# Value products on the transposes' banks, in two halves per head, and score tiles on three slots without a break

## The reference, cut to what matters

```
scores = q k^T                        per head: [256, 16] x [16, 4096]
p      = softmax(scores)              over the 4096 keys
pq     = round(p * 255 / max(p))      0..255, scale kept aside
vq     = round(v / scale_v)           -127..127, one scale per channel
o      = (pq @ vq) * scales           [256, 4096] x [4096, 16] per head
x      = x + o @ Wp + bp
```

## Time and profile before

| | us |
|---|---|
| median of 3 runs | 864.43 (859.89 to 864.85) |
| profiled execution | 861.99 |
| its span, first to last instruction | 860.0 |
| mean granted TensorE clock | 0.899 of full speed |
| busy in the span: PE, DVE, ACT, POOL | 688.4, 546.8, 416.0, 313.9 |

### The profile page before, as it was taken

How to read it: one execution, slowest core, us unless ns; L and a number is a source line. 1 busy time by engine, 2 the same in 40 slices (tenths; PEclk the granted TensorE clock), 3 DMA queues, 4 the chain that set the end, 5 groups by cost and what they waited for, 6 DMA issues and landing times. The chain is left out here.

```text
span 860.0 us, 14159 instructions
## 1 busy us (share of the span) xinstructions
PE 688.4 (80%) x4484; PEld 453.1 (53%) x4484; DVE 546.8 (64%) x834; ACT 416.0 (48%) x759; POOL 313.9 (36%) x232
## 2 busy tenths in 40 slices
PE   3817899978999998789974776867858676899997
PEld 1413445445776766567741444544535455576775
DVE  4487999955222222699986888788788883534222
ACT  2225555513222222355544888788788883313221
POOL 0081788850000000144432766666666662000000
PEclk9967999979999999899995889688797977999999
DMA  8554000003343430334437424224224200860000
GB/s 354 232 198 195 1 0 0 0 1 115 111 165 110 165 110 0 105 95 129 125 91 147 69 37 74 37 37 73 37 37 69 41 0 1 320 270 1 1 0 12
DMA packets 28652, 76.65 MB, mean 89 GB/s; under 512 B 3472, under 2 KB 21072, under 8 KB 22224
## 3 DMA queue, kind: packets, MB, share of 16 engines
q1 hardware_dynamic: 16080, 70.00, 27.7%
q10 hardware_dynamic: 12544, 6.29, 2.6%
HBM read 69.66 MB, written 6.62 MB: 89 GB/s over the span
## 5 line engine op out<-in xcount | busy, mean ns | idle before, releaser
L1468 DVE TENSOR_REDUCE d_nmax<-d_psum 128x1024 f32 (+1 forms) x128 | 155.4, 1217 | 15.1 <-PE d_psum L1595 12.0
L1605 PE MATMUL d_psum<-d_ident_f,d_rounded 128*128 128x128 f16 x1024 | 98.2, 253 | 64.5 <-ACT d_probsT L1551 62.6
L1605 PEld LDWEIGHTS d_psum<-d_ident_f,d_rounded 128*128 128x128 f16 x1024 | 81.4, 115 | 119.9 <-issue 82.6
L1595 PE MATMUL d_psum<-d_kst,d_qT 96*128 96x512 bf16 x256 | 98.4, 475 | 14.2 <-DMA d_kst<-kT_scratch 8.2
L430 POOL TENSOR_TENSOR b_h<-b_h,b_cb 128x1024 f32<-128x1024 f32 x32 | 84.5, 2642 | 31.4 <-DVE b_h L484 31.0
L1539 ACT ACTIVATE d_e<-d_psum,d_nmax 128x1024 f32<-128x1024 f32 x64 | 71.3, 1113 | 40.5 <-DVE d_nmax L1468 36.2
L1447 POOL TENSOR_SCALAR d_rounded<-d_e,d_lift 128x1024 f16<-128x1024 f32 x64 | 72.4, 1132 | 45.3 <-ACT d_lift L1543 40.9
L1447 POOL TENSOR_SCALAR d_rounded<-w_early,d_lift 128x1024 f16<-128x1024 f32 x64 | 71.6, 1119 | 40.4 <-ACT d_lift L1543 29.2
L484 DVE TENSOR_TENSOR_SCAN b_h<-b_dA,b_psum 128x1024 f32<-128x1024 f32 x32 | 73.0, 2285 | 7.6 <-PE b_psum L588 4.8
L544 ACT ACTIVATE b_dA<-b_dtT,b_A 128x248 f32<-128x248 f32 x128 | 53.6, 490 | 49.3 <-DVE b_h L484 43.3
L1539 ACT ACTIVATE w_early<-d_psum,d_nmax 128x1024 f32<-128x1024 f32 x64 | 71.2, 1114 | 8.6 <-DVE d_nmax L1468 8.5
(11 more groups left out here) (372 smaller groups left out, 1195.9 us busy)
## 6 DMA issues: line engine op xcount, KB each, us to landing
d_kst<-kT_scratch SPq DMA_DIRECT2D x96, 128.0 KB, 4.5
w_early<-in_w SPq DMA_DIRECT2D x8, 1152.0 KB, 5.2
w_late<-in_w SPq DMA_DIRECT2D x8, 1152.0 KB, 5.2
w<-in_w SPq DMA_DIRECT2D x8, 1088.0 KB, 19.9
b_cb<-c_scratch SPq DMA_DIRECT2D x4, 2048.0 KB, 7.1
kT_scratch<-k_kT ACTq DMA_DIRECT2D x16, 384.0 KB, 2.8
a_ctxT<-in_ctxT SPq DMA_DIRECT2D x2, 2048.0 KB, 11.8
a_ctx<-in_ctx SPq DMA_DIRECT2D x2, 2048.0 KB, 20.3
```

Of the source, the lines that this page charges most:

```text
L1468: nc.vector.tensor_reduce(nm[:, t, ds(m, 1), f:f + 1], quarter(j).unsqueeze(1), AX.X, ALU.max, negate=True).then_inc(nm_ready, 1)
L1595: last = nc.tensor.matmul(quarter(j)[:, c * 512:(c + 1) * 512], qT[0:QROWS, ds(m, 1), t * P:(t + 1) * P], kst[s][0:QROWS, at:at + 512], st ...
L1605: last = nc.tensor.transpose(turned[j % 2][:, c * P:(c + 1) * P], r[j][:, c * P:(c + 1) * P], ident16[:, :])
```

## The change

The value products move from banks 4 and 5 to the two banks of the turns: the uses of these banks now form a ring per head, T0, T1, V, T2, ..., T7, which alternates between them (nine uses, so the parity changes from head to head), and every use waits until the use two before it has been read. V is issued in two halves, tile 0 behind T1, tile 1 between S2 and T2, and `finish` reads 32 neighbouring columns of one bank, behind copy 2. The score units rotate over the three slots without regard to heads, so a score pair waits for the exp three units back. The slots and banks repeat after six heads, so the loop body holds six rounds and four rounds run ahead of it. `pT` and `vh` are f16. The scale of the values is computed in round 0 behind search 2. GpSimd fills a small constant tile (`unlift`) behind the all-reduce, and TensorE waits for that before its first score; the tile is read only by units turned by DMA, of which there are none here (`BY_DMA` is empty). SP's key loads are unrolled.

```diff
-    SLOT = (0, 1, 0, 1, 2, 0, 1, 2)
-    AV_BANK = 4
+    BY_DMA = ()
+    BY_PE = tuple(j for j in range(APH) if j // QT not in BY_DMA)
+    EVEN = tuple(j for j in BY_PE if j % 2 == 0)
+    ODD = tuple(j for j in BY_PE if j % 2 == 1)
+    RING = tuple(j for j in BY_PE if j < 2) + ("values",) + tuple(j for j in BY_PE if j >= 2)
     TURN_BANK = 6
+    UNROLL, LEAD = 6, 4
...
-        r = [sb(f"d_rounded{j}", [P, QUARTER], F16) for j in range(APH)]
-        pT = [sb(f"d_probsT{s}", [P, TC, NKC, P], BF16) for s in range(2)]
+        r = [sb(f"d_rounded{t}", [P, NK], F16) for t in range(TC)]
+        pT = [sb(f"d_probsT{s}", [P, TC, NKC, P], F16) for s in range(2)]
+        unlift = sb("d_minus_1024", [P, P], F16)
...
-            for m in range(2):
-                body(m, m, 0)
-            with eng.Fori(1, H // 2) as i:
-                for s in range(2):
-                    body(i * 2 + s, s, i)
+            for m in range(LEAD):
+                body(m, m, m // 2)
+            with eng.Fori(0, (H - LEAD) // UNROLL) as i:
+                for c in range(LEAD, LEAD + UNROLL):
+                    body(i * UNROLL + c, c, i * (UNROLL // 2) + c // 2)
...
+            slot = (c * APH + j) % 3
+            return flat[:, slot * QUARTER:(slot + 1) * QUARTER]
+
+        def turn_bank(c, use):
+            return TURN_BANK + (c * len(RING) + RING.index(use)) % 2
...
                 nc.gpsimd.partition_all_reduce(vall[:, :], g["vam"][:, :], P, RMAX).then_inc(vall_ready, 1)
+                nc.gpsimd.memset(unlift[:, :], -HALF_ULP_ONE).then_inc(ident_ready, 1)
...
+                def vector_head(m, c, i):
                     for j in range(APH):
                         if live(m, 0, H):
-                            search(m, j)
-                        if j % 2 == 0 and live(m, 1, H + 1):
-                            copy_even(m, s, j)
-                        if j == 1 and live(m, 2, H + 2):
-                            finish(m)
+                            search(m, c, j)
+                        if isinstance(m, int) and m == 0 and j == 2:
+                            value_scale()
+                        if j in EVEN and live(m, 1, H + 1):
+                            copy_even(m, c, j)
+                        if j == 2 and live(m, 2, H + 2):
+                            finish(m, c)
...
-                pe.wait_ge(ident_ready, 1)
+                pe.wait_ge(ident_ready, 2)
...
-                    if j == 4 and live(m, 2, H):
-                        pe.wait_ge(o_ready, m - 1)
...
-                        before = {0: -2, 1: -1, 2: 1, 3: 2, 5: 3, 6: 4, 7: 5}[j]
...
+                    if live(m, 1, H) or j >= 3:
+                        pe.wait_ge(e_ready, m * APH + (j - 2))
...
+                def bank_free(m, use):
+                    at, back = RING.index(use) - 2, 0
+                    while at < 0:
+                        at, back = at + len(RING), back + 1
+                    before = RING[at]
+                    if before == "values":
+                        if live(m, 2 + back, H + 2):
+                            pe.wait_ge(o_ready, m - (1 + back))
+                    elif live(m, 1 + back, H + 1 + back):
+                        copied, some = ((even_copied, EVEN), (odd_copied, ODD))[before % 2]
+                        pe.wait_ge(copied, m * len(some) + (some.index(before) + 1 - (1 + back) * len(some)))
...
+                def values(m, c, t):
+                    out = ps[:, turn_bank(c, "values"), t * HD:(t + 1) * HD]
...
+                def tensor_head(m, c, i):
                     for j in range(APH):
                         if live(m, 0, H):
-                            scores(m, s, i, j)
-                        if live(m, 1, H + 1):
-                            turn(m, j)
+                            scores(m, c, i, j)
+                        if j == 2 and live(m, 2, H + 2):
+                            values(m, c, 1)
+                        if j in BY_PE and live(m, 1, H + 1):
+                            turn(m, c, j)
                         if j == 1 and live(m, 2, H + 2):
-                            values(m, s)
+                            values(m, c, 0)
```

More of the change, by code:

```diff
@@ L1362, in xattn1_stage @@
         turn_psum = sem("d_turn_psum")
+        turned_in = [sem(f"d_turned_in{t}") for t in range(TC)]
         even_copied = sem("d_even_copied")
@@ L1417, in _, with turn_unit @@
                 sp.dma_start(g["w_inT"][:, :, :], d["w_inT"]).then_inc(g["w_inT_in"], 16)
[L1419 to L1425, removed]
+                def turn_unit(m, t):
+                    sp.wait_ge(r_ready, m * APH + (t + 1) * QT)
+                    if m >= 2:
+                        sp.wait_ge(av_done, m + 1)
+                    sp.dma_start_transpose(pT[m % 2][:, t, :, :], r[t][:, :]).then_inc(turned_in[t], 16)
+                for m in range(H):
+                    if 0 in BY_DMA:
+                        turn_unit(m, 0)
+                    if m + 2 < H:
+                        sp.wait_ge(scores_ready, m * APH + APH)
+                        load_keys((m + 2) * HD, m % 2)
+                    if 1 in BY_DMA:
+                        turn_unit(m, 1)
             @block.gpsimd
@@ L1599, in turn @@
[L1599 to L1606, removed]
@@ new lines, in turn @@
+                def turn(m, c, j):
+                    pe.wait_ge(r_ready, m * APH + (j + 1 - APH))
+                    bank_free(m, j)
+                    for b in range(CPQ):
+                        last = nc.tensor.transpose(turn_tile(c, j)[:, b * P:(b + 1) * P], tile_of(r, j)[:, b * P:(b + 1) * P],
+                                                   ident16[:, :])
+                    last.then_inc(turn_psum, 1)
+                def values(m, c, t):
+                    out = ps[:, turn_bank(c, "values"), t * HD:(t + 1) * HD]
+                    if t == 0:
+                        bank_free(m, "values")
+                        pe.wait_ge(vh_ready, m - 1)
+                    if t in BY_DMA:
+                        pe.wait_ge(turned_in[t], m * 16 - 16)
+                    else:
+                        pe.wait_ge(even_copied, m * len(EVEN) - len(EVEN))
+                        pe.wait_ge(odd_copied, m * len(ODD) - len(ODD))
+                    for b in range(NKC):
+                        last = nc.tensor.matmul(out, pT[c % 2][:, t, b, :], vh[c % 2][:, b, :], start=(b == 0),
+                                                stop=(b == NKC - 1 and t not in BY_DMA))
+                        if t in BY_DMA:
+                            last = nc.tensor.matmul(out, unlift[:, :], vh[c % 2][:, b, :], start=False, stop=(b == NKC - 1))
+                    if t == TC - 1:
+                        last.then_inc(av_done, 1)
```

103 lines of the change are left out of this document (46 added, 57 removed).

## The result

The changed kernel takes 879.3 us (median of 6 runs, 875.81 to 881.72), the kernel before 861.04 beside it (858.46 to 864.85): ratio 1.0197, 95% interval 1.016 to 1.0235, so 2.0% slower. The prediction stood on the 864.43 of the kernel before's first three runs. The profiled execution took 876.04, its span is 874.3, the mean granted clock 0.876 (before 861.99, 860.0, 0.899).

A forecast was written before the change was run, and what follows sets the result against it. It took a ring of waits through several engines, with neither VectorE nor ScalarE full, to set the round. The terms +0.65 + 1.85 - 0.3 + 12 x 0.5 + 0.7 = +8.9 beside 864.43 gave 873 us, range 861 to 881.

The forecast's parts named there:

- The forecast of the ring: T2's new wait for ScalarE's copy 1 sets the rounds: +5 to +14 us, the case forecast, chance 0.48.
- The shared banks, the new wait: In each round T2 waits for ScalarE's copy 1 behind exp 1: 15.98 us at full clock against 15.51.
- The value products split: In each round S2 comes 0.81 us earlier and finish no longer waits; read alone, 14.85 us against 15.51.
- At the lower clock: Looped rounds pay 0.85 us when T2 is slow, 8 of 14 times; mean round about 16.5, +0.5.
- The larger loop body: The longer hardware loop body and SP's unrolled key loads cost nothing; bounds -1 to +2 us.
- Rounds 2 and 3: These rounds leave the hardware loop, where search 3 to search 4 takes longer, counted twice a round: -0.3 us.
- The drain: In the drain, T3 right behind T2 waits for copy 2 and finish: about +0.7 us.
- `value_scale`, round 1: Scaling moved behind search 2 delays head 0's search 3, +0.65 us; in round 1 T2 waits for copy 1, +1.85.
- f16 values: f16 loads cost the value products 0; as a rival, slow loads cost +12 in all, 885 us, chance 0.05.
- The new memset: At the start on GpSimd: 0.2 us, hidden by the keys; as a rival, +5.2, 878 us, chance 0.08.
- Rival 1: In the rounds, the wait for V was the whole limit: round 14.85, 855 down to 845 us, chance 0.09.
- Rival 2: T2's wait holds but meets full clock: rounds 15.9 to 16.2, +1 to +5, 865 to 869 us, chance 0.30.

The follow-up runs named there:

- the kernel with the added products: The changed kernel with two products of 384 columns, read by nobody, behind V's second half in each round; 873.7 us, ratio 1.0136 to the kernel before.
- copy 1 first: The changed kernel with ScalarE's copy 1 ahead of exp 1 in its queue; 860.58 us, ratio 0.9999 to the kernel before.

## Why the prediction was right in kind and short in size

It said +8.9 with a range up to 881; the change costs +18.3 by the medians, +15.8 by the stage of the trace. That 879.3 lies inside the range owes something to luck: 881 is 16.6 above the 864.43 that it started from, and the kernel before took 861.04 beside the changed one. The forecast of the ring was "+5 to +14", and the cost is above it. By its own steps:

- **The shared banks, the new wait**: right. Every link stands in the timeline, and breaking it gives back 18.7 us in the loop. The walk to 15.98 less up to 0.1 at full clock can be tried on the kernel with the added products: of its looped rounds with a T2 of 0.61 two last 15.83, one 16.06.
- **The value products split**: right. 6.6 us when done alone, `finish` without idle, the shortest rounds 14.81 where the walk had 14.85.
- **At the lower clock**: mis-sized; this is the first step that failed. It took a mean round of 16.5, with 8 of 14 T2 at the lower level. Measured is 16.75 without the jump, +0.76 on 15.99 where it had +0.5. The price of 0.85 was about right for the loop: a round with T2 at the lower clock lasts 0.66 more (16.49 against 15.83), where later turns and scores are at it too 1.13 more (16.96), on average 0.92. In straight code it is 0.57. What was wrong is the share: all twelve T2 in the loop meet the lower clock. It assumed that the clock would stay as it was; it went from 0.81 to 0.75, and in straight code to 0.87. That the longer waits of TensorE bring this about was shown in part: with work put into them the clock rose to 0.82 and 0.39 a round came back. The loop has a part as well: of the T2 in rounds 4 to 15 twelve are at the lower clock with the wait and the loop, nine with the loop alone (copy 1 first, clock 0.82), six with the wait alone (no loop, 0.87).
- **"The larger loop body … I cost at nothing … Bounds -1 to +2"**: wrong. 3.4 us here, 9.8 in the kernel before given the same loop. "Straight-line rounds show no gap" spoke of another thing: the gap lies at the jump.
- **Rounds 2 and 3**: -1.32, not -0.3. Outside the loop the ring does better than the same rounds before. The step counted the slower tiny operations twice a round, 0.66. Search 3 to the end of the next search 1, "the unbroken 11.99", takes 10.24 + 1.21 = 11.45 in straight code, 0.54 less, in rounds at either clock; what search 4 gains behind search 3 at full clock goes into a longer `round_values` (0.97 in place of 0.50).
- **The drain**: +2.54, not +0.7. T3 behind `finish` is the largest part and was right in kind: T3 starts 1.99 behind T2 where it was 0.81, +1.18. The other 1.4 is 0.46 up to T2 (T1 lasts 1.01 in place of 0.61) and 0.90 behind T3, where T5, T6 and T7 last 1.01 or 1.06 in place of 0.61. Copy 1 is no part of it: with copy 1 first T2 starts 3.90 behind the lift, as in the changed kernel. In straight code the drain costs +1.6, again with 1.18 at T3.
- **`value_scale`, round 1**: +0.60 (search 0 to the second lift, 12.93 against 12.33) and +1.70 (15.08 against 13.39), where it had +0.65 and +1.85.
- **Three score slots** at 0: nearly; without them +4.1.
- **f16 values** at 0: right. Each half of V, 32 products, takes 0.95 to 1.05, and S2 starts 0.81 after V's first product (676.21 to 677.02), 25 ns a pair, as in bf16. The Trainium skill, "TensorE: Matmul & The Clock Gate", section "Weight-path perf modes", which gives the fast load to every 128-column weight but fp32 ones, agrees.
- **The new memset** at 0: right. On GpSimd:

```profile
455.94 1.15 POOL L1455 PARTITION_ALL_REDUCE d_v_absmax<-v_absmax  x1 [12.64 <-issue]
456.97 0.28 POOL L1456 MEMSET d_minus<- 128x128 f16 x1
466.95 1.25 POOL L1463 TENSOR_TENSOR d_vh_scaled<-v,d_v_rscale 128x512 f32<-128x512 f32 x1 [9.69 <-DVE d_v_rscale L1493]
```

It follows the all-reduce at once, and search 0 is at 461.38. The delay of some 6 us that the Trainium skill, GPSIMD Engine Reference, section "Instruction dispatch", gives for a first call doesn't reach a memset here.

The prediction read all of the 7.89 before the first scaling as a delay. 2.1 of it was the wait for the reciprocal, which ends at 457.92 + 1.75 = 459.67; for the other 5.8, to 465.45, that wait was over. In the changed kernel the reciprocal runs later, and there the scaling follows its end at once:

```profile
465.10 1.75 DVE L1493 RECIPROCAL d_v_rscale<-d_v_scale 128x256 f32<-128x256 f32 x1
```

It ends at 466.85, and GpSimd starts at 466.95. Whether the 5.8 passed unseen during the longer wait, or the memset had something to do with it, no run here tells.

The terms sum to +0.60 + 1.70 - 1.32 + 12.26 (12 rounds, the jump in them) + 2.54 = +15.8, all of the stage's difference. Rival 1 (faster) fell with its condition: copy 1 ends 2.33 after search 1 (676.80 to 679.13). By its own terms its lower end was 842, not 845 (864 + 14 x (13.9 - 15.5)). Rival 2, that the ring meets full clock, holds in straight code only, and there in every other round.

**What stays open**: why TensorE needs 3.5 us at one jump and 9.4 at another, with the same number of rounds in the body; and what in the loop brings the lower clock to T2, as the counts of twelve, nine and six are of one trace each.

## What to carry to other kernels

When a buffer comes to be shared, write down whose read the next user now waits for, and what stands ahead of that read on its engine: here a copy of 1.01 us behind an exp of 1.11. Moving that one copy gave back 18.7 us in the loop, and 2.9 in straight code. Time a change of order apart from a change of the loop around it: the split alone wins 6.6 us, the longer body alone loses 8.2, and together with the shared banks the result tells nothing of either. Where a ring of waits runs in a hardware loop, time it as straight code too: that gave 7.6 us to the kernel before and 21.6 to the changed one, and left 3.7 between them. Don't price a slow short operation by the number of times that it occurs: it costs where its engine sets the ring, and nothing where the next operation waits for another engine anyway.

## What the runs showed of the hardware that was not expected

- A jump back over a body of six rounds, with 864 products (6 x 144) and as many weight loads a pass, left TensorE idle for 3.5 to 9.4 us once in each of five kernels, with nothing to wait for in the profile. The two-round loop shows nothing of that size in seven passes: its longest round is 16.42.
- From a search over the two tiny operations behind it to the start of the next search takes 1.84 us (behind search 3, kernel before) to 1.88 (behind search 7, changed kernel) in a loop and 1.51 outside it.
- Unread products shortened the rounds by 0.39 us each on average, at a clock of 0.82 in place of 0.75.
- GpSimd's first scaling started 5.1 to 6.1 us after the reciprocal that it waits for in the five kernels that compute the reciprocal ahead of round 0, and 0.09 to 0.10 after it in the seven that compute it behind search 2.
